# Feeding a gated linear recurrence by DMA instead of by selecting matmuls, with a new order of the front of a decoder layer

## The reference

```python
# branch 1: gated linear attention, 16 heads, 8 key and 16 value columns each
q, k, v = x @ Wq, x @ Wk, x @ Wv                      # 128, 128, 256 columns
gk = log_sigmoid(x @ Wgk1 @ Wgk2 + bgk2) / 16
h = h * exp(gt)[..., None] + kt[..., None] * vt[..., None, :]    # scan over the 1024 tokens
ot = einsum('bhk,bhkv->bhv', qt * scale, h)
o = rmsnorm(o) * gnw * silu(x @ Wg);  x = layernorm(x + o @ Wo)
# branch 2: attention of every token to 64 of its batch's 64 context rows, with repeats
c_sel = (ctx @ W_kv_down.T)[indices]                  # indices (2, 1024, 64)
x = layernorm(x + softmax(q k / 4) v @ W_out.T)
# branch 3: causal attention over 1024 tokens, then 8 experts (top 2 of the router, 1024 wide)
x = layernorm(x + block(x))
```

## Time and profile before

| | before |
|---|---|
| median of 3 runs | 1351.96 us (1350.18 to 1352.32) |
| profiled execution, its own time | 1351.55 us |
| its span in the profile | 1349.5 us |
| PE busy | 1280.6 us (95%) |
| PE weight loads busy | 957.5 us (71%) |
| DVE busy | 936.8 us (69%) |
| ACT busy | 626.0 us (46%) |
| POOL busy | 277.6 us (21%) |
| granted TensorE clock, mean | 0.984 of full speed |
| front block | 0 to 196.3 us |

### The profile page before, as it was taken

One profiled execution on the slowest core, in us unless ns is written; L12 is line 12 of the kernel. 1 busy time (PEld: TensorE's weight loads), 2 busy tenths in 40 slices (PEclk: granted clock), 3 DMA queues, 4 the chain that ended last, 5 costly groups with the idle time before them and its releaser, 6 DMA issues.

```text
span 1349.5 us, 19595 instructions
## 1 busy us (share of the span) xinstructions
PE 1280.6 (95%) x7802; PEld 957.5 (71%) x7802; DVE 936.8 (69%) x1442; ACT 626.0 (46%) x936; POOL 277.6 (21%) x297
## 2 busy tenths in 40 slices
PE   8888769998999999999999999999999999999997
PEld 6555447767755555558888788888888888888886
DVE  7898767886889989758676655655656555555566
ACT  6677563265378778874342332323323233233233
POOL 8788961001334334210000000000000000000000
PEclk9899979999999999999999999999999999999999
DMA  5000001004612212212000120201101101010001
GB/s 141 1 1 1 0 1 36 1 1 170 191 48 60 57 52 60 75 39 72 17 2 16 30 73 16 71 16 39 47 9 53 34 28 59 16 39 16 1 17 47
DMA packets 40330, 55.81 MB, mean 41 GB/s; under 512 B 9552, under 2 KB 26624, under 8 KB 40240
## 3 DMA queue, kind: packets, MB, share of 16 engines
q1 hardware_dynamic: 35056, 43.67, 10.7%
q0 software_dynamic: 3648, 10.09, 2.6%
q10 hardware_dynamic: 1536, 0.81, 0.2%
HBM read 43.73 MB, written 10.55 MB: 40 GB/s over the span
## 4 chain that ended last, share of the span: by engine, by line
PE 52%; DVE 2%; ACT 0%; issue 0%; ACTq 0%; DVEq 0%
PE PS L2602 25%; PE PS L2615 25%; PE PS L2365 1%; PE PS L114 0%; PE PS L2628 0%; PE PS L2346 0%; PE PS L2379 0%; DVE OT_all L2763 0%; DVE r_st L2441 0%; DVE r_on L2458 0%; DVE r_on L2438 0%; PE PS L2640 0%; DVE X L2450 0%; DVE x_mid L2754 0%; ACT X L2724 0%
## 5 line engine op out<-in xcount | busy, mean ns | idle before, releaser
L2685 ACT ACTIVATE x_g<-PS,x_bias 128x512 f32<-128x512 f32 x256 | 175.8, 687 | 493.4 <-PE PS L2602 493.3
L2602 PE MATMUL PS<-x_h,x_w 128*128 128x512 f32 x1536 | 398.7, 395 | 0.0
L2615 PE MATMUL PS<-x_mid,x_w 128*128 128x512 f32 x1488 | 384.0, 393 | 1.1 <-DVE x_w L2337 1.1
L2602 PEld LDWEIGHTS PS<-x_h,x_w 128*128 128x128 f32 x1536 | 286.1, 188 | 64.7
L2615 PEld LDWEIGHTS PS<-x_mid,x_w 128*128 128x128 f32 x1488 | 279.2, 188 | 65.7 <-DVE x_w L2337 1.6
L2754 DVE CAST x_mid<-x_g 128x512 fp32r<-128x512 f32 x256 | 109.2, 427 | 266.4 <-ACT x_g L2685 266.0
L2204 DVE TENSOR_REDUCE a_M<-PS 128x2 f32<-128x1024 f32 (+1 forms) x144 | 173.1, 1223 | 24.2 <-PE PS L1901 18.0
L2756 DVE TENSOR_TENSOR x_mid<-x_g,x_mid 128x512 fp32r<-128x512 f32 x256 | 177.2, 692 | 8.8
L2142 ACT ACTIVATE f_parts<-PS 128x512 f32<-128x512 f32 x224 | 120.8, 601 | 35.9 <-PE PS L1955 24.9
L2582 POOL DMA_DIRECT2D x_wb<-route_w x31 | 16.8, 541 | 477.0 <-DVE OT_all L2763 453.7
L231 POOL TENSOR_TENSOR qh<-qh,QT 128x1024 f32<-128x1024 f32 x31 | 73.5, 2376 | 17.2 <-DVE qh L574 17.2
(11 more groups left out here) (405 smaller groups left out, 1641.9 us busy)
## 6 DMA issues: line engine op xcount, KB each, us to landing
x_raw<-L_ffn_e_w SPq DMA_DIRECT2D x32, 512.0 KB, 3.8
qk_parts<-f_parts SPq DMA_DIRECT2D x16, 512.0 KB, 2.9
x_wb<-route_w POOLq DMA_DIRECT2D x31, 256.0 KB, 3.4
aQ<-qk_parts SPq DMA_DIRECT2D x96, 64.0 KB, 2.5
aK<-qk_parts SPq DMA_DIRECT2D x60, 64.0 KB, 2.6
X<-x SPq DMA_DIRECT2D x4, 512.0 KB, 7.5
aK<-qk_parts SPq DMA_DIRECT2D x36, 48.0 KB, 2.0
out<-X SPq DMA_DIRECT2D x3, 512.0 KB, 3.5
```

Of the source, the lines that this page charges most:

```text
L2602: last = e.matmul(PS[:, f % 2, :], w1[n % 2][u][:, kt, f * P:(f + 1) * P], self.rows(v, k)[:, kt, :], start=m == 0 and kt == 0, stop=m == ...
L2615: last = e.matmul(PS[:, 2 + 2 * (it % 2) + d, :], w2[n % 2][v][:, f, d * P:(d + 1) * P], mid[u][:, f % RM, :], start=f == 0 and m == 0, st ...
L2685: e.activation(g[s % RG][:, :], PS[:, f % 2, :], ACT.Gelu, bias=b1[:, n, f:f + 1]).then_inc(A.sem, 1)
```

## The change

1. **Values by DMA.** `sel`, `values` and the split of the values are gone. DVE (first) or ACT copies the turned values in float32 to `vT`. SP issues one DMA for each step from SBUF to SBUF: row j of each head, repeated on the head's 8 rows, 512 KB, into a ring of 4 slots `vring`.
2. **Keys in PSUM.** The keys of the batch at hand stay in banks 2 and 3 (for batch 1 ACT copies them there from `KT`, behind product 15). The product reads `vring` and the keys and writes banks 0 and 1, always the same ones, so it waits for the scan before.
3. **Counting.** POOL makes 7 indicators (n = 11, 19, ... 59) instead of 17, now as -0.5 and 0.5 so that no correction is needed; ACT makes 58 signs instead of 48.
4. **Key blocks.** ACT makes the high part in eight strips straight from `kT` (L828 of the new kernel), POOL the low one; `Kblk` between them is gone.
5. **Order.** The slots of ACT and PE stand in one written-out list without `jj`; POOL's and DVE's branches are at other steps. In the tail, the turn of tile 0 stands before the second half of tile 1's product, the splitting of the query weights is in the loop, the statistics of tile 1 are behind it.

The diff, cut to its core:

```diff
-        self.QT, self.KT, self.decay = sb("QT", [P, N]), sb("KT", [P, N]), sb("decay", [P, N])
+        self.QT, self.KT, self.decay = sb("QT", [P, N]), sb("KT", [P, T]), sb("decay", [P, N])
+        self.vT = sb("vT", [P, 2, T])
...
+        VR = 4
+        s_vb = [self.sem(f"gs_vb{n}") for n in range(VR)]
...
-        of_scalar = [n for n in range(NCTX) if n % 4 < 3]
+        pooled = (11, 19, 27, 35, 43, 51, 59)
+        of_scalar = lambda first, last: [n for n in range(first, last) if n not in pooled]
...
             @block.sync
...
+                for jj in range(NJ):
+                    n, j = jj // DK, jj % DK
+                    e.wait_ge(s_hi, n + 1)
+                    if jj >= VR:
+                        e.wait_ge(s_kv, jj - VR + 1)
+                    e.dma_start(self.vring[:, jj % VR, :], self.vT[j:P:DK, n % 2, :].unsqueeze(1).broadcast_to((H, DK, T))).then_inc(s_vb[jj % VR], 16)
             @block.gpsimd
...
-                    n = 4 * u + 3 if u < 16 else NCTX
-                    e.tensor_scalar(hot[:, n % RS, :], self.idxT[:, :], float(3 * 16 + u), None, ALU.is_ge).then_inc(s_hot, 1)
+                def indicator(n):
+                    e.wait_ge(s_cnt, (n - RS) // 4 + 1)
+                    e.tensor_scalar(hot[:, n % RS, :], self.idxT[:, :], float(context(n)), 0.5, ALU.is_ge, ALU.subtract).then_inc(s_hot, 1)
...
                 for jj in range(NJ - 1):
                     output(e, jj)
...
+                    if jj in (4, 7, 10, 15, 19, 22, 25):
...
+                    elif jj == 23:
+                        self.out_gated_pool(e, 0, s_gate)
+                    elif jj == 24:
+                        self.out_gated_pool(e, 1, s_gate)
+                    elif jj == 26:
+                        e.wait_ge(V.sem, V.at("klo"))
+                        e.wait_ge(S.sem, S.at("G3"))
+                        for b in range(B):
+                            for g in range(KD):
+                                keys_lo(b, g)
+                    elif jj == 29:
                         self.out_rows_pool(e, 0, s_row)
-                indicator(16)
                 self.out_rows_pool(e, 1, s_row)
             @block.tensor
...
-                def values(jj):
-                    n, j = jj // DK, jj % DK
-                    if jj >= 2:
-                        e.wait_ge(s_h, jj - 1)
...
             @block.vector
...
                 def product(jj):
-                    e.wait_ge(s_v, jj + 1)
-                    if jj == HD:
-                        e.wait_ge(A.sem, A.at("k1"))
-                    e.tensor_tensor(wide(2 * (jj % 2)), wide(2 * (jj % 2)), KT[:, batch(jj // HD)], ALU.mult).then_inc(s_kv, 1)
+                    e.wait_ge(s_vb[jj % VR], 16 * (jj // VR + 1))
+                    if jj:
+                        e.wait_ge(s_h, jj)
+                    if jj == 0:
+                        e.wait_ge(S.sem, S.at("k0"))
+                    elif jj == HD:
+                        e.wait_ge(A.sem, A.at("k1b"))
+                    e.tensor_tensor(wide(0), self.vring[:, jj % VR, :], wide(2), ALU.mult).then_inc(s_kv, 1)
                 def state(jj):
...
-                    e.tensor_tensor_scan(qh[:, jj % RQ, :], decay[:, batch(jj // HD)], wide(2 * (jj % 2)), 0.0, ALU.mult, ALU.add).then_inc(s_h, 1)
+                    e.tensor_tensor_scan(qh[:, jj % RQ, :], decay[:, batch(jj // HD)], wide(0), 0.0, ALU.mult, ALU.add).then_inc(s_h, 1)
...
             @block.scalar
...
-                def parts_hi(n):
+                def values_copy(n):
                     e.wait_ge(s_vt, n + 1)
                     if n >= 2:
-                        e.wait_ge(s_v, DK * (n - 1))
-                    e.activation(vparts[:, 0, n % 2, :], wide(vt_banks(n)), ACT.Copy).then_inc(s_hi, 1)
+                        e.wait_ge(s_kv, DK * (n - 1))
+                    e.activation(self.vT[:, n % 2, :], wide(vt_banks(n)), ACT.Copy).then_inc(s_hi, 1)
...
+                e.wait_ge(s_kv, HD)
+                e.activation(wide(2), KT[:, :], ACT.Copy).then_inc(A.sem, 1)
```

More of the change, by code:

```diff
@@ L394, in _ @@
                 both(Wkp, 2)
-                values(0)
                 both(Wqp, 6)
@@ new lines, in _ @@
+                sums(0)
+                counts(2)
+                turn(0)
+                e.wait_ge(s_tok, 2)
+                low(1, 4)
+                counts(3)
+                e.wait_ge(A.sem, A.at("low1"))
+                sums(1)
+                counts(4)
+                turn(1)
+                e.wait_ge(s_tok, 4)
+                gate(4)
+                counts(5)
+                e.wait_ge(A.sem, A.at("z1"))
+                turned_values(2)
+                counts(6)
+                e.wait_ge(s_hi, 3)
@@ new lines, in _ @@
+                for x, src in enumerate((self.down, self.ctx)):
+                    for k in range(KD):
+                        last = e.transpose(PS[:, 5, (KD * x + k) * P:(KD * x + k + 1) * P], src[:, 0, k * P:(k + 1) * P], ident[:, :])
+                last.then_inc(S.sem, 1)
+                e.wait_ge(A.sem, A.at("udc"))
+                sums(5)
+                turn(5)
+                e.wait_ge(s_tok, 12)
+                for kt in range(KD):
+                    last = e.matmul(PS[:, 4, 0:P], downT[:, kt, :], ctxT[:, kt, :], start=kt == 0, stop=kt == KD - 1)
@@ L528, in _ @@
+                last.then_inc(S.sem, 1)
+                counts(14)
+                e.wait_ge(A.sem, A.at("khi"))
+                e.wait_ge(V.sem, V.at("keys"))
+                self.out_product(e, 0, SB, (0, 1))
+                counts(15)
+                self.out_product(e, 0, SB, (2, 3))
+                counts(16)
+                e.wait_ge(self.OA[0].sem, self.OA[0].at("y"))
+                sums(6)
                 e.wait_ge(s_fin, 1)
```

581 lines of the change are left out of this document (253 added, 328 removed).

## The result

The changed kernel takes **1337.74 us** (median of 4 runs, 1337.06 to 1339.05), the kernel before 1352.14 (4 runs beside them, 1350.18 to 1352.69): ratio 0.9898, 95% interval 0.9886 to 0.9909, 14.4 us faster. Forecast were 1335.0 us and 1322 to 1348. The profiled execution has a span of 1335.3 us, 14.2 less than before.

A forecast was written before the change was run, and what follows sets the result against it. The front was taken as bound by VectorE with its waits for PE up to 172 us, then GpSimd's backlog and small steps to 196.3. Terms -0.9 + 0.4 - 9.4 - 6.7 = -16.6 us gave 1335.0 us, range 1322 to 1348.

The forecast's parts named there:

- Start: Up to the first product: fewer VectorE steps, but a wait for the first 512 KB transfer; -0.9 us, bounds -1.5 and +3.7.
- VectorE's work: Recurrence: subtractions and a statistic leave, weights' parts and a key subtraction enter, products wait for scans; together +0.4 us.
- Transfers in the loop: Ring of 4 in the recurrence: 2.9 us transfers hidden under about 13 us of cover; cost 0.
- Idle time: VectorE's waits in the recurrence fall from 22.8 to 13.4 us; -9.4 us, bounds -22.8 and +5.
- The walk: Four new engine orders stepped through side by side, giving VectorE 7.4 us idle with TensorE at full speed.
- The 6 us added for the low clock: Recurrence: four of ten TensorE groups at the lower clock level cost 1.5 us each on the path.
- ten indicators at 2769 ns: Work GpSimd loses, 27.7 us, leaving it no indicator behind step 25.
- Tail: From the last scan to the front block's end: 17.7 us instead of 24.4; -6.7 us, bounds -10 and 0.
- GpSimd is busy without a gap before: Sign for the last scan: if GpSimd has no gap before it, the forecast is wrong.
- the low clock: Rival: TensorE's low clock level replaces the wait for L340 in the recurrence; 1343.3 us, chance 0.18.
- The loose ring: Rival: PE and ScalarE keep ahead and the clock holds, idle 3 instead of 22.8 us; 1322.9 us, chance 0.14.
- the GpSimd rival: Rival: GpSimd's late outputs stay the bound and scans wait for head sums; 1350 us, chance 0.06 with handed-on waits.

The follow-up runs named there:

- the fillers: Changed kernel with 58 matmuls of a weight of zeros added at nine places of TensorE's queue, so that it is seldom idle; 1333.6 us.
- run bseven: Kernel before, with ten of GpSimd's seventeen indicators left out and values still chosen by matmuls; 1342.6 us.
- run six: Changed kernel with the indicator of context 59 moved from GpSimd to ScalarE as a sign; 1337.9 us.
- best: Changed kernel, weights' parts in the tail, context 59 on ScalarE, tile 1's squares before signs 47 to 49, one-operation indicators with constant removed; 1332.33 us, ratio 0.9858.
- bestwarm: The kernel of best with the 58 added zero-weight matmuls on TensorE; 1330.29 us, ratio 0.9833 against the kernel before.

## Why the prediction was right, point by point

The time is 2.7 us above the forecast. The mechanism is as foreseen in the main: the waits for L340 are gone, the transfers are hidden, the tail is shorter. The last scan was to end near 162 and does, at 162.0, but that it does so to the tenth is luck: inside that sum three terms missed, by 6.5 us one way and 6.2 the other.

- **Start** (-0.9, bounds -1.5 and +3.7): +0.2. The transfer takes 4.5 us from its issue to landing, not the 2.9 of the store in the earlier trace rows. The step that failed is the choice of the nearest row, and not for the queue: with one slot, and so one transfer at a time, landing takes 4.2 us too.
- **VectorE's work** (+0.4): +5.8 on the same count. Its busy time between first product and last scan is 127.7 us (90.58 and 37.12) for 125.3 (85.77 and 39.56), and between a scan and the next product there is now a gap of 0.11 us, 31 times, 3.4. The wait for the scan costs 0.19 us a step instead of 0.13 (scan to product 2.39 to 2.40 for 2.20 us), 5.9 in all for 4.0. The weights' parts were priced at 1.2 us from the tail, where GpSimd is idle, and cost 6.5 beside it, 5.3 more. That is the term that was most wrong: a duration was carried to a place with another neighbour. The scan's wait adds 1.9 more than priced, and nearly as much went the other way, among it two things that no term counted: the copy of batch 1's keys (1.2 us) is now ScalarE's, and the second gate subtraction takes 1.5 us for 2.5. So the step is off by 5.4.
- **Transfers in the loop** (0): right in outcome. They land after 4.3 us, not 2.9, with 13 us of cover. Behind the first product none is waited for; with one slot the waits are 54 us and the last scan is 42 us later.
- **Idle time** (13.4 us for 22.8): 7.2, the last scan's 138.3 us behind the first product less 127.7 busy and 3.4 of gaps. The walk alone had said 7.4, and had the places: means of tile 1 4.0 and measured 3.5, last step 1.8 and 1.9 (for the rows of tile 0, not for their deviation), first decay 0.3 and 0.9; only the low parts of x, 1.3, are not waited for. The 6 us added for the low clock are the mistake: the fillers give back 3.2, 1.9 of it by the wait for the squares, which I had counted apart. This term is 6.2 us better than its step, the start and VectorE's work together 6.5 us worse. A slip that changed nothing: ScalarE's busy time up to 172 us is 111.4 us by the earlier trace rows, not 112.4; it became 128.8, not some 124.
- **GpSimd** (ten indicators at 2769 ns, 27.7 us fewer): the seven left cost 0.86 more each, 6 us. The second operation was in the diff, and I took the old duration for it. It matters: with one operation the last scan ends 3.5 us earlier. That relief of GpSimd is a source of its own, run bseven shows; but I had put all 13.8 us of VectorE's waits down to L340's place in the queue, and 2.8 of them go by that relief alone.
- **Tail** (17.7, -6.7): 19.4, -5.0. Output 31 was priced at 1.4 and takes 3.44 beside GpSimd's output 30. Through VectorE's and ScalarE's next steps (L621, L840) it delays the copy of tile 1, which ends 7.1 us behind the last scan for 5.6 in the sum. Another 1.5 us pass between GpSimd's rows (done at 179.96) and the next block (181.45), a step for which the sum had no term. The steps between are 0.8 us shorter, and the 0.6 us for a cold TensorE did not come in this execution, whose tail has a clock of 1.00.

Of the signs named ahead: products 1.23 us, under 1.25, and 2.40 us behind the scan's start, not 2.3; ScalarE 107 of 130 us busy, over 80%; clock 0.87, under 0.93; block end 181.4, within 175 to 185; landing under 13 us. Idle time of VectorE was to be 10 to 17 us, most for ScalarE and head sums: it is 10.6 with the gaps in front of the products and 7.2 without them, nearly all for ScalarE and none for head sums. One sign was too coarse: "GpSimd is busy without a gap before" the last scan was to refute the forecast. It has a gap of 3.7 us there (156.2 to 159.9), so the sign did not come; but GpSimd is busy without one from 119.3 to 142.8 us and does hold the counts, which the sign does not see.

Of the rivals the low clock had the right mechanism and too high a price (1343.3; the fillers give back 3.2 us of the block and 4.1 of the time, with 0.93 still short of full speed). The loose ring (1322.9) is not there even with fillers and all edits, which give 1330. That the last scans wait for head sums, as in the GpSimd rival, is not seen; its bound came in by the counts.

## What to carry to other kernels

Price an instruction with what will run beside it. A 128x128 cast of 0.22 us took 2.37 because a GpSimd instruction on SBUF had begun just before, so VectorE's short casts, and its operations on two operands in SBUF, belong where GpSimd is idle; reciprocals and statistics lost nothing here. When an edit on the path buys almost nothing, look for a second chain into the same instruction and cut both: 0.4 and 1.2 us apart were 5.6 together with a third edit. Before you believe 1 us of a single run, look where in the trace it arises: that of run six was there 20 us ahead of its edit. And a change that takes work from two engines at once should be tried by its halves: here the half without any new data path, work taken off GpSimd, had up to 7.6 of the 14.4 us.

## What the runs showed that I had not expected

- VectorE's casts, subtractions and multiplications from SBUF to SBUF end at most one length of their own behind the GpSimd instruction that was running: 1.84 for 0.42 us, 2.31 for 0.69, 2.37 for 0.22, 3.44 for 1.36. Products with one operand in PSUM are not touched (1229 ns, 32 times), nor are reciprocals and statistics. The Trainium skill, "SBUF — State Buffer", "Who interferes with whom", has this as an exclusive lock held for a whole instruction; the trace agrees. GpSimd loses too, if less: 2.69 us at 134.13 for the 2.36 that L904 takes elsewhere.
- GpSimd's comparison of 1024 bf16 columns takes 2.77 us, and 3.63 with a second operation in the instruction. On ScalarE the sign takes 1.14.
- A transfer of 512 KB that repeats 16 rows of SBUF over 128 lands after 4.3 us, at 203 to 223 GB/s when several are queued, and after 4.2 us when it is alone; from 16 neighbouring rows after 7.2.
- The same 16 head-sum matmuls in the tail, behind 2.0 us of idle TensorE, take 1.92 us in best's trace and 3.60 in bestwarm's. This alone moves the end of the block by up to 1.7 us from one trace to the next.
